# Merged attention and expert stage: an own order for the first five turns, expert blocks one step earlier, one burst of scatters per group; GRU tail norm later

## The reference, cut to what matters

```python
x = x + _L0_gnn_ref(_layernorm(x), adj, W, a)      # graph attention, 128 graphs of 64 nodes, width 128
x = x + _L0_ffn_ref(_layernorm(x), ...)            # 8 experts, hidden 512, each token goes to its best 2
x = x + _L1_gnn_ref(_layernorm(x), adj, ...)       # gated graph net: 3 layers of messages and a GRU cell
x = x + _L1_ffn_ref(_layernorm(x), ...)            # 16 experts, hidden 256, top 2

def _L0_gnn_ref(input, adj, W, a):
    h = input @ W
    e = leaky_relu(s1[:, :, None] + s2[:, None, :], 0.2)      # s1, s2 = h @ a1, h @ a2
    attention = softmax(where(adj > 0, e, NEG_BIG), axis=2)
    return elu(attention @ h)
```

## Time and profile before

| what | us |
|---|---|
| median of 3 runs (lowest, highest) | 1101.84 (1100.24, 1102.51) |
| the profiled execution, its own time | 1102.61 |
| its span, first to last instruction | 1100.9 |
| PE, DVE, ACT, POOL busy | 961.4, 764.9, 550.7, 595.9 |

### The profile page before, as it was taken

The page is one execution under the profiler, slowest core; times in us unless marked ns, Lnnn a source line. Parts: engine busy times, 40 slices in busy tenths (PEclk is TensorE's granted clock), DMA queues, the critical chain, the costliest instruction groups (busy, mean ns, idle before and its releaser), DMA issues. The chain is left out here.

```text
span 1100.9 us, 24163 instructions
## 1 busy us (share of the span) xinstructions
PE 961.4 (87%) x6368; PEld 777.4 (71%) x6369; DVE 764.9 (69%) x2968; ACT 550.7 (50%) x1356; POOL 595.9 (54%) x625
## 2 busy tenths in 40 slices
PE   4567999999997899399999999999993899999970
PEld 3456999999987799345555555555552899999970
DVE  4446888888884466448888888888875555555558
ACT  3545556656643234145655656655643444444455
POOL 2145677777777555301155454545535777766670
PEclk9666999999998899799999999999995999999995
DMA  9601222222222221222032130340011643333349
GB/s 225 213 30 54 81 88 71 71 72 87 72 70 87 72 80 56 72 72 77 1 104 83 38 104 21 105 125 28 25 44 35 139 126 103 88 96 87 92 154 363
DMA packets 101512, 99.36 MB, mean 90 GB/s; under 512 B 32412, under 2 KB 86300, under 8 KB 101148
## 3 DMA queue, kind: packets, MB, share of 16 engines
q1 hardware_dynamic: 84252, 62.83, 20.5%
q0 software_dynamic: 17152, 35.29, 9.2%
HBM read 55.44 MB, written 42.62 MB: 89 GB/s over the span
## 5 line engine op out<-in xcount | busy, mean ns | idle before, releaser
L430 POOL DMA_INDIRECT queue<-rows,slots x256 | 261.5, 1022 | 177.1 <-issue 73.4
L2145 POOL DMA_INDIRECT result<-e_y,e_ids x144 | 143.8, 998 | 57.1 <-issue 47.6
L1001 POOL DMA_INDIRECT result<-a_y,a_ids x136 | 133.3, 980 | 76.2 <-issue 38.4
L2176 PE MATMUL e_ps_h<-e_xT,e_up_of 128*128 128x128 f32 x1152 | 143.0, 279 | 2.8 <-DVE e_hT L2289 2.8
L2176 PEld LDWEIGHTS e_ps_h<-e_xT,e_up_of 128*128 128x128 f32 x1152 | 136.6, 195 | 3.6 <-issue 3.2
L1480 PEld LDWEIGHTS a_ps_y<-w_sb,a_hT 128*128 128x128 f32 x1088 | 134.0, 196 | 4.5 <-issue 1.3
L1480 PE MATMUL a_ps_y<-w_sb,a_hT 128*128 x1088 | 135.0, 279 | 1.1 <-DVE a_y L1161 1.1
L1464 PE MATMUL a_ps_up<-a_xT,a_up_of 128*128 128x256 f32 x448 | 111.6, 395 | 0.0
L2289 DVE TENSOR_TENSOR e_hT<-e_ps_h,e_gate 128x512 f32<-128x512 f32 x72 | 49.7, 690 | 73.1 <-ACT e_gate L2224 71.6
L1464 PEld LDWEIGHTS a_ps_up<-a_xT,a_up_of 128*128 128x128 f32 x448 | 84.5, 199 | 9.8
L2224 ACT ACTIVATE e_gate<-e_ps_h 128x512 f32<-128x512 f32 x72 | 43.0, 597 | 96.7 <-PE e_ps_h L2176 96.7
(11 more groups left out here) (271 smaller groups left out, 2122.4 us busy)
## 6 DMA issues: line engine op xcount, KB each, us to landing
xq<-queue SPq DMA_DIRECT2D x168, 64.5 KB
g_y<-result SPq DMA_DIRECT2D x20, 512.0 KB, 4.1
xq<-queue SPq DMA_DIRECT2D x56, 129.0 KB
x_res<-x SPq DMA_DIRECT2D x16, 256.0 KB, 3.8
w_sb<-w SPq DMA_DIRECT2D x2, 2048.0 KB, 12.5
queue<-rows,slots POOLq DMA_INDIRECT x256, 2.8
w_sb<-w SPq DMA_DIRECT2D x16, 256.0 KB, 4.1
rows<-result SPq DMA_DIRECT2D x8, 512.0 KB, 8.1
```

What stands on the lines that cost most here:

```text
L430: pool.indirect_dma_start(out=queue, out_offset=bass.IndirectOffsetOnAxis(ap=c.slots[q][:, k, t:t + 1], axis=0), in_=c.rows[q][:, k, t, :] ...
L1001: pool.indirect_dma_start(out=c.result0, out_offset=bass.IndirectOffsetOnAxis(ap=ids[slot.k][:, t, :].bitcast(U32), axis=0), in_=y[slot.k] ...
L2145: pool.indirect_dma_start(out=result, out_offset=bass.IndirectOffsetOnAxis(ap=ids[at_down.k][:, t, :].bitcast(U32), axis=0), in_=y[at_down ...
L2176: last = pe.matmul(ps_h[b][:, t, q * P:(q + 1) * P], up_of[at_up.k % 4][:, t, q * P:(q + 1) * P], xT[at_up.k % 4][:, t, :], start=True, st ...
```

## The change

1. Turns T < EARLY = 5, which have no expert blocks, get an order of their own on VectorE, ScalarE and TensorE. Their gate scores and ranks go to another PSUM bank (`ps_y`).
2. In every turn `project` computes the attention scores (`ps_s`) ahead of the projection (`ps_h`).
3. FIRST_SLOT goes from 22 to 21: all expert slots stand one quarter earlier, slots 0, 4, 8, ... in quarter 1.
4. GpSimd sends the 8 scatters of a group in one burst in quarter 1, behind the results of that quarter, and no longer two in each quarter ahead of them.
5. VectorE makes the batch's table a little earlier in the turn.
6. In the GRU block the tail norm of the pair's first half moves on ACT from the end of step 1 into step 2, and on PE its transposes move behind the two state matmuls of the gates.

```diff
-FIRST_SLOT = 22
+FIRST_SLOT = 21
+EARLY = 5
...
             for T in range(turns):
                 for j in range(FOUR):
-                    s = group(T - 2 if j else T - 3)
-                    if s is not None:
-                        send_rows(s, 2 * (j - 1) if j else 6)
                     at_down = stages(T, j)[2]
                     if at_down:
                         send_results(at_down)
+                    if j == 1 and group(T - 2) is not None:
+                        send_rows(T - 2)
...
# VectorE
+                if T < EARLY:
+                    stats_1(next_g)
+                    aggregate(norm1, VN1, next_g)
+                    if before_g is not None:
+                        update(before_g)
+                    shift(norm1, VN1, AN1, next_g)
+                    if before_g is not None:
+                        wait(v, VU, "x1", before_g)
+                        stats(norm2, VN2, before_g)
+                        aggregate(norm2, VN2, before_g)
+                    mask(next_g)
+                    attend(g)
+                    if before_g is not None:
+                        shift(norm2, VN2, AN2, before_g)
+                    if two_back is not None:
+                        route(two_back)
+                    mixed(g)
+                    if two_back is not None:
+                        place(two_back)
...
# ScalarE
+                if T < EARLY:
+                    copy_turned("x", g, xnT)
+                    inverse_std(norm1, VN1, AN1, next_g)
+                    normalise_1(next_g)
+                    if before_g is not None:
+                        inverse_std(norm2, VN2, AN2, before_g)
+                    copy_e(g)
+                    exps(g)
+                    copy_h(g)
+                    copy_turned("p", g, pT)
+                    if before_g is not None:
+                        normalise_2(before_g)
+                        copy_turned("r", before_g, rT)
+                        copy_rows(before_g)
+                    elus(g)
+                    continue
...
# TensorE, project(s)
-                wait(pe, VU, "z", s - 1)
-                wait(pe, VS, "scores", s - 2)
-                for t in range(G):
-                    last = pe.matmul(ps_h[:, t * D:(t + 1) * D], xnT[:, t * P:(t + 1) * P], w_sb[:],
-                                     start=True, stop=True)
-                last.then_inc(QX.sem, 1)
                 wait(pe, VM, "neg", s)
                 wait(pe, AE, "e", s - 1)
...
+                wait(pe, VU, "z", s - 1)
+                if s >= EARLY:
+                    wait(pe, VS, "scores", s - 2)
+                for t in range(G):
+                    last = pe.matmul(ps_h[:, t * D:(t + 1) * D], xnT[:, t * P:(t + 1) * P], w_sb[:],
+                                     start=True, stop=True)
+                last.then_inc(QX.sem, 1)
...
# GRU block, TensorE and ScalarE
-                if inside:
+                if inside and l == 0:
                     inside()
                 after(pe, s_z, u, 1)
                 pe.matmul(ps_r[:], c.w_hh[:, 0:D], h[:], start=True, stop=False)
                 pe.matmul(ps_z[:], c.w_hh[:, D:2 * D], h[:], start=True, stop=False)
+                if inside and l:
+                    inside()
...
+                    if k == 2 and has_tail:
+                        norm_tail(pa[0])
                     if has_run:
                         agg_out(n, l, b)
...
-                    if k in (1, 2) and has_tail:
-                        norm_tail(pa[k - 1])
+                    if k == 2 and has_tail:
+                        norm_tail(pa[1])
```

More of the change, by code:

```diff
@@ L819, in gat_and_experts @@
         pairs = DOUBLES + SINGLES // PAIR
-        turns = (pairs + 2 + FIRST_SLOT) // FOUR
+        turns = -(-(pairs + 2 + FIRST_SLOT) // FOUR)
         tables = TokenTables(nc, ctx, c, E0)
@@ L866, in gat_and_experts, with scores_at, ranks_at @@
         ps_h = ps_o[:, 0, :]
-        scores_ps = ps_o[:, 0, 0:G * E0]
-        ranks_ps = ps_o[:, 1, 0:(G + 1) * E0]
+        def scores_at(s):
+            return ps_y[:, 0:G * E0] if s + 2 < EARLY else ps_o[:, 0, 0:G * E0]
+        def ranks_at(s):
+            return ps_y[:, G * E0:G * E0 + (G + 1) * E0] if s + 2 < EARLY else ps_o[:, 1, 0:(G + 1) * E0]
         half_o = ps_o[:, :, 0:2 * (D + 1)].rearrange("p b (j d) -> p b j d", j=2)
@@ L988, in _, with send_rows @@
             make_constants(pool, c)
[L990 to L995, removed]
+            def send_rows(s):
+                wait(pool, VK, "slots", s)
+                wait(pool, AC, "rows", s)
+                alone(pool, c)
+                queue_rows(pool, c, c.queue0, s % TURN)
             def send_results(slot):
@@ L1109, in place @@
             def place(s):
-                carry = c.carry[:, 0:E0]
+                carry, ranks_ps = c.carry[:, 0:E0], ranks_at(s)
                 wait(v, QK, "ranked", s)
@@ L1178, in _ @@
                 batch = T - 4
+                if T < EARLY:
[17 more added lines that the diff above has]
+                        place(two_back)
+                    if batch == 0:
+                        wait(v, VK, "carried", batch + 2)
+                        tables.doubles_1(v, c)
+                        tables.doubles_2(v, c)
+                        tables.doubles_3(v, c, batch)
+                    continue
                 now, at_up, at_down = stages(T, 0)
@@ L1200, in _ @@
                     aggregate(norm2, VN2, before_g)
+                if 0 <= batch < tables.batches:
+                    wait(v, VK, "carried", batch + 2)
+                    tables.doubles_1(v, c)
                 if T == NG + 2:
@@ L1217, in _ @@
                 if 0 <= batch < tables.batches:
-                    wait(v, VK, "carried", batch + 2)
-                    tables.doubles_1(v, c)
+                    tables.doubles_2(v, c)
                 now, at_up, at_down = stages(T, 3)
@@ L1399, in score_rows @@
                 pe.wait_ge(turned_out, turn_of["r", s] + 1)
-                wait(pe, VU, "z", min(s + 1, NG - 1))
+                if s + 2 < EARLY:
+                    wait(pe, VK, "carried", s - 1)
+                else:
+                    wait(pe, VU, "z", min(s + 1, NG - 1))
+                scores_ps = scores_at(s)
                 for t in range(G):
@@ L1428, in rank_rows @@
                 wait(pe, VK, "carried", s - 1)
+                ranks_ps = ranks_at(s)
                 pe.matmul(ranks_ps, c.before[:], both[:].rearrange("p t e -> p (t e)"), start=True, stop=False)
@@ L1438, in mix @@
                 wait(pe, AH, "h", s)
-                wait(pe, VK, "carried", s - 2)
+                if s >= EARLY:
+                    wait(pe, VK, "carried", s - 2)
                 for t in range(G):
@@ L1486, in _ @@
                 g, before_g, two_back = group(T), group(T - 1), group(T - 2)
+                if T < EARLY:
+                    wait(pe, AN1, "normed", g)
+                    turn_in("x", g, xn)
+                    project(g)
+                    wait(pe, AA, "exp", g)
+                    turn_in("p", g, pbd)
+                    if two_back is not None:
+                        score_rows(two_back)
+                    mix(g)
+                    if before_g is not None:
+                        wait(pe, AN2, "normed", before_g)
+                        turn_in("r", before_g, rows[before_g % TURN][:, 0, :, 0:D])
+                    if two_back is not None:
+                        rank_rows(two_back)
+                    continue
                 if g is not None:
```

8 lines of the change are left out of this document (3 added, 5 removed).

## The result

The changed kernel takes 1094.5 us (median of 4 runs, 1093.53 to 1095.5) where the kernel before takes 1101.88 in the same comparison; the ratio is 0.993 with a 95% interval of 0.991 to 0.995. It is faster by 7.4 us. The profiled execution took 1093.53 us with a span of 1091.8, against 1102.61 and 1100.9.

What follows compares the result with a forecast made beforehand. It took PE and POOL as full in the ten expert turns, with the new burst closing a loop. Merged stage +5.7 us and GRU -6.2 took 1102.61 to 1102.1, 1101.6 as a median; range 1092 to 1109.

Steps and rivals of the forecast that it cites:

- the loop: Slots 4 to 44: burst waits for quarter 1's addition, next turn's slot for the burst; 21.9 us, turns of 22.0.
- The rival of a shorter loop: Full turns: DMAs and landing overlap more, turns of PE's 20.7 us; 1083 us in all, chance 0.18.
- the mean pace: Burst on POOL: rival with 1.33 us a DMA, turns of 22.5 us; 1107.5 us in all, chance 0.24.
- the low price: Burst on POOL: 1.26 us a DMA, since DVE's update in quarter 0 would not stand beside the burst.
- The Trainium skill's rule on float32 copies: Burst: rival that DVE's matrix copies hold up scatters by 0.5 us each; turns of 23.5, 1117 us, chance 0.04.
- Two engines are full: Slots 4 to 44 before the change: PE busy 20.5 us a turn, POOL's 16 DMAs 21.3 at 1.33 apiece.
- The tail: Slots 44 to 52: PE runs at half clock after waits, two loops of 24.7 us, costing 5.2 us.
- The early turns: Turns before expert slots: new order gives 14.2 us for 17.3; turn 5 near 78 us, slot 0 at 93.3.
- the prediction's own sign: Stated test at the first expert slot: the prediction is wrong if slot 0 comes outside 90 to 97 us.
- faster, if PE gets its full clock: Early turns: rival saving 2.5 us a turn, slot 0 5 us earlier; 1096 us in all, chance 0.17.
- Cost nothing: Turns 5 and later: scores ahead of the projection and the earlier table priced at zero, PE being full there.
- GRU: GRU stage: moving the tail norm removes PE's waits for `g_tok`, saving 6.2 us, bounds 3 and 6.4.

Runs made afterwards that it cites:

- e1: Changed kernel with FIRST_SLOT back at 22, every expert slot one quarter later; 1073.53 us.
- e2: Changed kernel with the eight scatters sent ahead of quarter 1's results instead of behind them, FIRST_SLOT still 21; 1074.2 us.
- e8: Changed kernel with the scatters again two per quarter, the last two in quarter 0 of the next turn, FIRST_SLOT 21; 1152.17 us in one run.
- e6: Kernel before with only the one-burst scatters behind quarter 1's results, FIRST_SLOT 22; 1092.31 us.
- e4: Changed kernel with the GRU edit taken back; 1102.19 us.
- e10: Kernel before with only the attention scores moved ahead of the projection; 1084.11 us.
- e3: Changed kernel with EARLY = 0, so the first five turns keep the later turns' order; 1091.03 us.
- e11: Changed kernel with EARLY = 0 and the eight scatters ahead of quarter 1's results, FIRST_SLOT 21; 1071.69 us.
- e12: Changed kernel with EARLY = 0 and FIRST_SLOT = 22; 1073.78 us.
- e5: Kernel before with the GRU edit alone; 1096.13 us.

## Why the prediction came out as it did

**What bounds the kernel, and the loop: right, to 0.2 us.** 21.9 us round the loop was forecast and 21.71 is in the rows, with parts of 4.52, 0.78, 12.34 and 4.07 for 4.5, 0.8, 12.3 and 4.2. The ten turns are 21.94 each where 22.0 stood. e1, e2 and e8 show the loop itself: opened, shortened and lengthened, it takes 21 and 20 us away and puts 58 on. The rival of a shorter loop is out. So is the mean pace: the long DMA went with the update, as the low price assumed. In after most of the long results lie beside it (from 100 to 330 us the 19 results that overlap its two passes take 1.12 us in the mean, the 41 that overlap neither a pass nor a copy 0.96), and in the first burst the one long scatter at 77.34 does:

```profile
77.21 0.68 DVE L1085 SCALAR_TENSOR_TENSOR a_xz<-a_z,x_res 128x512 f32<-128x512 f32 x1
77.93 0.69 DVE L1088 SCALAR_TENSOR_TENSOR x_res<-a_elu,a_xz 128x512 f32<-128x512 f32 x1
```

The Trainium skill's rule on float32 copies (SBUF — State Buffer, "SBUF: two separate sides") would have made the burst slow. The trace does not bear that out for the burst: from 100 to 330 us in after, the 24 scatters that overlap a copy of a slot's matrix take 0.97 us in the mean, as the others do (0.96). For single DMAs it agrees in a small size, which the prediction had not seen: a result that starts just behind the start of a copy takes 1.20 us.

```profile
241.25 0.43 DVE L1136 COPY a_up_of<-w_sb 128x512 f32 x1 [0.28 <-issue]
241.31 1.20 POOL L1006 DMA_INDIRECT result<-a_y,a_ids  x1 [0.30 <-issue]
```

In e2, where other results meet the copies, 10 of the 21 beside one take 1.10 to 1.19 us.

**"Two engines are full": POOL was not.** The 1.33 us apiece hold waits: of the 45.8 us of idle time in the earlier trace rows, 6.8 end with DVE's addition or its places. And in e2 the same 16 DMAs fit a turn of 20.89 us. What kept before's turns above 21 us were five waits for `xq` of 0.5 to 1.0 us up to slot 40, 3.4 us in nine turns; e6, which has none of them, gains 2.8. The sum did not suffer by it, since the loop was priced by itself, but the reading hid that the kernel before already lost time to the same landing.

**The tail: right mechanism, one term too large.** A turn there was to be 24.7 us and is 23.73 and 23.72. The term that was off is the way from the slot's transposes to the end of its addition, 7.4 forecast, 6.20 measured (327.67 to 333.87), mostly by PE's clock: the granted clock behind this wait is 0.69, and 0.58 in the slot of before that the 7.4 were read from. +3.2 came instead of +5.2 up to slot 52, and behind that slot 0.9 us were gained that the sum had at nothing.

**The early turns: the step that was mis-sized.** "Turn 5 starts near 78 us" was 72.58, and slot 0, forecast at 93.3, came at 88.25; it was to be inside 90 to 97, so by the prediction's own sign this step was wrong. Part of the 5.4 us belongs to the single run: e1, e2, e4 and e8 have the same order on PE, DVE and ACT in turns 0 to 4 and reach turn 5 at 75.15, 76.46, 76.09 and 73.19, and slot 0 comes at 92.16 in e2, 91.78 in e4 and 88.69 in e8. In e1's turn 4 the transposes and the gate scores are at the lower clock (0.50 granted from 68.97 to 71.60; 0.86 in after from 67.46 to 69.10):

```profile
68.97 1.12 PE L1440 MATMUL a_ps_t<-ident,a_pbd 128*128 128x128 f32 x4 [1.36 <-ACT a_pbd L1331]
69.88 1.71 PE L1451 MATMUL a_ps_y<-a_gw,a_rT 128*128 128x8 f32 x8
```

1.12 and 1.71 us where after has 0.66 and 1.07; that is the whole difference between e1's turn of 13.80 us and after's 12.76. So the walk through the chain (14.2) was 0.4 too long for turn 4 at the lower clock, and the rival "faster, if PE gets its full clock" came true in part. That rival gave 1096, the nearest of all to the result; the range reached down to this time because of it. It had counted on 2.5 us a turn from the clock, and turn 4 got 1.0, so its number is in part luck. The other half of this step, that the gain is eaten by a wait ahead of slot 0, was right: 10.61 us of wait for 9.

**"Cost nothing" was right for the turns with expert blocks and hid the best part of the change.** The scores ahead of the projection were costed at nothing in turns 5 and later. In those turns they are worth a quarter of a microsecond each (e10). But the prediction gave the whole gain of the early turns to their new order, and never asked what the moved scores would do there alone. e10 answers: 11.5 us up to slot 4, 18.4 in all. e3, e11 and e12 answer for the order: it adds nothing that shows, since group 2's places move by 1 us while the turns move by 9. The last 4.6 us of e10's gain, behind slot 40, are read and not tested: 0.5 is a shorter wait ahead of slot 44, and most of the rest is PE's clock after the waits, 5.9 us for 7.1 in slot 44 and, in slot 52, 3.78 us at a granted clock of 1.00 for 6.73 at 0.55. Such a clock differs between runs, so this part may be chance.

**GRU: right.** 6.2 us forecast; 5.0 to 5.6 between the profiles compared above, 6.4 and 7.7 by the medians.

**The sum.** Slot 4 came 5.6 us earlier than forecast (108.29 for 113.9), the stage from there to the last slot was 3.6 us shorter, and the part behind it 0.6 longer: together the 8.6 us by which the profiled execution missed 1102.1. What the change is made of, by the runs: before, 1101.9, less 18.4 for the scores first (e10) and 6.4 for the GRU edit (e5) is 1077.1. The burst takes off another 3.3, to e12's 1073.8, and not the 10.2 that it takes off alone; the turns of e10, e6 and e12 are all 21.0 to 21.1 us, so the same time can't be gained there twice. The table's earlier place is part of that step too; no run has it alone. The early order adds nothing (e1, 1073.5). And the slots a quarter earlier, with results and burst in one loop, give back 21.0: 1094.5. So the forecast had the loop at its right size and place. What it had too small was the gain ahead of slot 4, 6.6 us forecast and 12.2 measured, and it gave that gain to the new order where the runs give it to the moved scores. How the early order would do with places made in the middle of its turns stays open; it wasn't tried.

## What to carry to other kernels

When two engines look full, lay the loop through them out as one chain and price it; here it came out to 0.2 us, and moving one burst in front of two DMAs was worth 20 us. When a change has several edits, price each one alone in every stage where it acts, above all those that seem to cost nothing: an edit that is free where an engine is full can be the gain where the engines wait for one another. And a stage that ends in a wait for something made in its middle isn't shortened by making its turns shorter; look where the thing waited for is made.

## What the runs showed of the hardware

A wait of some 4 us on PE costs almost half its length again: after 4.25 us in e8 the next matrices ran at a granted clock of 0.62 (3.62 us for 1.89), and the turn grew by about 6 us for a wait of 4.3. Behind a wait of some 3 us it went either way: 3.62 us for the same matrices after 3.10 us in before, 1.89 after 3.15 us in e10. Waits of 0.5 to 1.3 us left them at 1.89.

The early turns of the same code differ by up to 4 us between profiled runs (turn 5 at 72.58 in after, at 76.46 in e2), with PE's rows at either level of its clock: 0.66 or 1.12 us for four transposes.

POOL issues results and scatters alike 1.26 us apart, start to start. One that starts inside DVE's two passes over `x_res` takes 0.98 to 1.47 us in after, where it takes 0.96 by itself; one that starts just behind the start of a copy of 128x512 takes up to 1.2.
